# Six attention layers on one core: row tiles of TensorE that hold one head instead of two

## The chip, the cores and the metric

The kernel runs on one core of a Trainium2 chip. Its time is the device time of one execution in microseconds (us); the median of three is given for the kernel before, and lower is better.

## What is computed

A batch of 16 sequences (256 rows of 256 numbers, float32) passes through six layers. Five are attention layers with 16 heads of 16 numbers: L0 (keys and values from a context of 120 rows, with a mask, layer norm after), L1 (the same context, layer norm after), SELF (causal self-attention on 256 rows, layer norm ahead), CROSS (the context again, layer norm ahead) and L3 (the context, weights quantized to three values, layer norm ahead). Between CROSS and L3 stands FFN, two linear layers with a ReLU. Each attention layer is, for each sequence and cut to its core:

```python
q = (x @ Wq + bq).reshape(B, S, 16, 16)
k = (c @ Wk + bk).reshape(B, C, 16, 16)
v = (c @ Wv + bv).reshape(B, C, 16, 16)
scores = jnp.einsum('bqhd,bkhd->bhqk', q, k) * 16 ** -0.5
probs = jax.nn.softmax(scores, axis=-1)
ctx = jnp.einsum('bhqk,bkhd->bqhd', probs, v).reshape(B, S, 256)
y = x + ctx @ Wo + bo
```

## The kernel before, in words

An item is one sequence in one layer: i = 16 x layer + sequence, 96 items, 80 of them of attention (0 to 15 are L0, 16 to 31 L1, 32 to 47 SELF, 48 to 63 CROSS, 64 to 79 FFN, 80 to 95 L3). In the layers other than SELF two neighbouring sequences share one load, one K and one V: their contexts lie beside each other as 240 columns.

An attention item goes through named stages. On TensorE: Q (projection, L549), K and V (L560, L572), A (scores with queries on the output partitions, for the maxima; L600, in SELF L612 and L622), M (transpose of the negated maxima, L634), B (scores with keys on the output partitions, L655 and L660), PV (L679 to L689), ON, OT (transposes, L699, L709), O (output projection, L718). A has one unit for each half of the queries (SELF: three units, since the causal mask leaves one quarter out), B one for each half of the heads (SELF again three). On the other engines: Qh and Ql write the rounded part of q (fp32r) and its rest from PSUM (L794 on ACT, L917 on DVE), K0, Kh and Kl do so for k (L804 and L815 on ACT, L925 on DVE), max takes the maxima from the scores (L966 on DVE), mTe copies the transposed maxima (L823 on ACT), exp is L839 and L841 on ACT.

A score is a product in three parts, as high x high + high x rest + rest x high (PARTS, line 12), so that fp32r products keep float32's precision. The products of A and B use the array as four row tiles of 32 rows each, so that four matmuls run beside each other. 32 rows hold two heads of 16. To get one head's scores, the keys lie in SBUF twice, once with the odd heads zeroed and once with the even heads zeroed: the tensor hsel, 1 or 0 for each partition, multiplies them in Kh and Kl. A unit of A is 24 matmuls (2 groups of heads x 3 parts x 4 row tiles) that each cover two heads, 240 columns. A unit of B is 24 matmuls of 256 columns (2 heads x 3 parts x 4 row tiles), and 8 more at L660 add the negated maxima, picked out of mT by a column of ones and zeros (pickr).

```python
e.matmul(banks[j][0:n, wide * x:wide * x + wide], kz[row[j], lk, g, c, k0:k0 + n], q[row[j], lq, g, qs_],
         start=(x == 0 and y_ == 0), stop=False)
...
t = e.matmul(banks[j][0:n, wide * x:wide * x + wide], pickr[row[j], 2 * g + c:2 * g + c + 1].to_broadcast([32, n]), mt[row[j], qs_],
             start=False, stop=(x == len(parts) - 1))
```

The order on each engine is fixed at build time. make_plan lists every stage with the stages that it follows, a wanted time (WANT, in items, added to i), a length (LONG, us) and for transfers a landing time (LAND); Plan.run plays these numbers through and writes down the order in which each engine takes its stages. Buffers are rings (Slots) and PSUM banks, given out in the same play. At run time each engine goes through its list in order and waits on semaphores; nothing overtakes. SP issues all transfers, in its own list.

## Time and profile before

| | before |
|---|---|
| median of 3 executions | 1464.22 us (1463.85 to 1464.83) |
| the profiled execution: its time, its span | 1464.82 us, 1463.1 us |
| TensorE matmul (PE) busy | 1404.4 us, 96% of the span |
| DVE, ACT, POOL busy | 1005.1, 783.9, 481.4 us |
| mean granted clock of TensorE | 0.991 |
| moved by DMA | 34.79 MB, 14000 packets |

The span runs from the first to the last instruction of the program on the core. Busy is the time in which at least one instruction of the engine was under way. An fp32 matmul of the source stands as two records in the trace (L549: 640 records for 320 matmuls), an fp32r matmul as one. Matmuls of different row tiles overlap, so what a stage costs is read from the start of its first matmul to the start of the next stage's, and not from the duration of one.

### The profile page before, as it was taken

The numbers are of one execution on the slowest core, as the hardware profiler recorded it, in microseconds if no ns is written. First come the engines' busy times: TensorE is split into PE (matmuls) and PEld (weight loads), VectorE is DVE, ScalarE is ACT, GpSimd is POOL, SyncE is SP. The second block draws the span as 40 slices with busy tenths as digits, with TensorE's granted clock in tenths as the row PEclk, the third lists the DMA queues.
The fourth block names the chain that finished last, engine by engine and source line by source line (L and its number), as shares of the span: only waits on it lengthen the run. The fifth ranks groups of instructions, "written<-read, shape, count | busy, mean of one in ns | idle before, by whom it ended". The sixth has DMA issues, their size and how long they took to land.

```text
span 1463.1 us, 42292 instructions
## 1 busy us (share of the span) xinstructions
PE 1404.4 (96%) x18408; PEld 1138.3 (78%) x18408; DVE 1005.1 (69%) x1895; ACT 783.9 (54%) x1305; POOL 481.4 (33%) x511
## 2 busy tenths in 40 slices
PE   4999999999999999999999999999989999899998
PEld 3777777777777777777777777778989999677775
DVE  3667677698787776666666677778686666656664
ACT  2565655655656555555555666665423334565663
POOL 6122213344444453332332221112485555000100
PEclk8999999999999999999999999999999999999999
DMA  7101000100000000000000100000000000000000
GB/s 290 37 26 43 23 26 15 52 9 16 9 9 9 31 16 2 2 2 2 2 2 16 45 9 9 15 9 23 30 1 1 2 1 8 16 30 30 30 24 30
DMA packets 14000, 34.79 MB, mean 24 GB/s; under 512 B 2167, under 2 KB 7543, under 8 KB 12407
## 3 DMA queue, kind: packets, MB, share of 16 engines
q1 hardware_dynamic: 13815, 32.09, 6.7%
...
## 4 chain that ended last, share of the span: by engine, by line
PE 82%; DVE 8%; ACT 5%; issue 2%; DMA 1%; POOL 1%; SPq 0%; DVEq 0%; ACTq 0%; POOLq 0%
PE ps L549 10%; PE ps L718 9%; PE ps L655 7%; PE ps L682 7%; PE ps L600 6%; PE ps L731 5%; PE ps L699 5%; PE ps L572 5%; PE ps L744 5%; PE ps L560 5%; ACT s_PU L841 4%; DVE s_nm L966 4%; PE ps L660 2%; PE ps L679 2%; PE ps L539 2%
## 5 line engine op out<-in xcount | busy, mean ns | idle before, releaser
L966 DVE TENSOR_REDUCE s_nm<-ps 128x8 fp32r<-128x960 f32 (+1 forms) x352 | 395.2, 1168 | 132.8 <-PE ps L600 74.8
L841 ACT ACTIVATE s_PU<-ps 120x1024 f32<-120x1024 f32 (+1 forms) x288 | 273.1, 1028 | 161.2 <-PE ps L660 161.2
L1105 POOL TENSOR_TENSOR s_xs<-s_xs,s_rowv 128x512 f32<-128x512 f32 x96 | 126.4, 1317 | 508.8 <-DVE s_nt L909 460.9
L655 PE MATMUL ps<-s_Qs,s_KH 32*120 32x256 f32 (+2 forms) x4608 | 180.3, 286 | 5.9 <-DVE s_xs L987 2.8
L655 PEld LDWEIGHTS ps<-s_Qs,s_KH 32*120 32x120 f32 (+1 forms) x4608 | 150.3, 181 | 41.2 <-issue 31.2
L549 PE MATMUL ps<-s_xT,s_W 128*128 128x256 f32 x640 | 163.4, 399 | 10.6 <-DMA s_xT<-x_t 9.4
L850 ACT ACTIVATE s_Os<-ps 128x512 f32<-128x512 f32 x160 | 94.4, 596 | 128.5 <-PE ps L682 83.4
L718 PE MATMUL ps<-s_W,s_oT 128*128 128x256 f32 x640 | 156.6, 387 | 1.3 <-ACT s_oT L857 0.9
L794 ACT ACTIVATE s_Qs<-ps,s_colv 128x256 fp32r<-128x256 f32 x160 | 67.2, 472 | 148.5 <-PE ps L549 148.5
L549 PEld LDWEIGHTS ps<-s_xT,s_W 128*128 128x128 f32 x640 | 118.2, 195 | 35.9 <-issue 11.1
L682 PE MATMUL ps<-s_PU,s_Vp 120*32 120x256 f32 x2048 | 126.3, 383 | 6.8 <-DVE s_nm L966 5.5
L718 PEld LDWEIGHTS ps<-s_W,s_oT 128*128 128x128 f32 x640 | 115.3, 190 | 20.8 <-ACT s_oT L857 2.4
L600 PEld LDWEIGHTS ps<-s_KH,s_Qs 32*128 32x128 f32 x3072 | 99.6, 185 | 34.4 <-issue 31.0
L600 PE MATMUL ps<-s_KH,s_Qs 32*128 32x240 f32 x3072 | 123.4, 290 | 1.4 <-DVE s_nm L966 1.4
L699 PE MATMUL ps<-s_ident,s_Os 128*128 128x128 f32 x640 | 100.4, 280 | 11.5 <-ACT s_PU L841 9.5
L987 DVE TENSOR_TENSOR s_xs<-ps,s_xs 128x512 f32<-128x512 f32 x96 | 66.2, 690 | 62.7 <-PE ps L718 56.4
L917 DVE SCALAR_TENSOR_TENSOR s_Qs<-ps,s_colv,s_Qs 128x256 fp32r<-128x256 f32 x160 | 69.7, 477 | 49.7 <-ACT s_Qs L794 49.7
L869 ACT ACTIVATE s_KH<-ps,s_c 128x256 fp32r<-128x256 f32 x128 | 50.3, 476 | 98.7 <-PE ps L731 98.7
L731 PE MATMUL ps<-s_Xs,s_W1s 128*128 128x256 f32 x768 | 100.3, 287 | 2.2 <-DVE s_PU L1034 2.2
L744 PE MATMUL ps<-s_W2s,s_KH 128*128 128x256 f32 x768 | 100.4, 288 | 0.5 <-POOL s_KH L1138 0.4
L1122 POOL TENSOR_SCALAR s_rs<-s_mv 128x2 f32<-128x2 f32 x96 | 21.4, 223 | 240.2 <-DVE s_mv L1003 237.5
L1138 POOL TENSOR_TENSOR s_KH<-s_PU,s_KH 128x1024 fp32r<-128x1024 f32 x32 | 76.7, 2397 | 69.0 <-DVE s_PU L1034 68.5
...
## 6 DMA issues: line engine op xcount, KB each, us to landing
...
s_W<-w_att SPq DMA_DIRECT2D x5, 1024.0 KB, 5.0
s_xs<-x_nat SPq DMA_DIRECT2D x4, 1024.0 KB, 11.8
s_xT<-x_t SPq DMA_DIRECT2D x16, 256.0 KB, 2.7
out<-s_xs SPq DMA_DIRECT2D x16, 256.0 KB, 2.0
...
s_W<-w_ff SPq DMA_DIRECT2D x2, 1024.0 KB, 5.1
...
```

The lines of the kernel that those rows point to most:

```text
L549: t = e.matmul(m[:, g * 256:g * 256 + 256], wv(layer, 0)[:, k, 128 * g:128 * g + 128], xT_of(i)[:, k, :], start=(k == 0), stop=(k == 1))
L600: t = e.matmul(banks[j][:, 240 * g:240 * g + 240].rearrange("p (c n) -> p c n", c=2), q[row[j], lq, g, 128 * u:128 * u + 128], kz[row[j], ...
L655: e.matmul(banks[j][0:n, wide * x:wide * x + wide], kz[row[j], lk, g, c, k0:k0 + n], q[row[j], lq, g, qs_], start=(x == 0 and y_ == 0), st ...
L682: t = e.matmul(o, vp[0:C, i % 2, 32 * h:32 * h + 32], p[0:C, j // 2, at:at + 256], start=True, stop=True, tile_position=(0, 32 * j))
L699: t = e.transpose(m[:, 256 * q + 128 * gr:256 * q + 128 * gr + 128], Os[slot("Os", (i, hf))][:, gr, 128 * q:128 * q + 128], ident[:, :])
L718: t = e.matmul(m[:, 256 * q:256 * q + 256], o[:, k, 128 * q:128 * q + 128], wv(layer_of(i), 3)[:, k, :], start=(k == 0), stop=(k == 1))
L731: t = e.matmul(o, W1[:, cw, k, 128 * mt:128 * mt + 128], x[:, cx, k, :], start=(c == 0 and k == 0), stop=(c == 2 and k == 1))
L744: t = e.matmul(m[:, 256 * q:256 * q + 256], hs[:, ch, k, 128 * q:128 * q + 128], W2[:, cw, 4 * hf + k, :], start=(hf == 0 and k == 0 and c ...
L841: t = e.activation(P_of(i, k)[0:n, :, :], pair("B", i, k)[0:n, :, :], ACT.Exp, scale=0.25)
L850: e.activation(o[:, :, :].rearrange("p a n -> p (a n)"), bankM("PV", i, hf), ACT.Copy).then_inc(sem["PVe"])
L966: e.tensor_reduce(o, v, AX.X, ALU.max, negate=True).then_inc(sem["max"])
L1105: e.tensor_tensor(xs[:, b, :, :], xs[:, b, :, :], row2(layer, 0), ALU.add).then_inc(sem["pool"])
```

## The change

Each row tile of 32 rows now holds one head. Its even rows hold the rounded part of the 16 numbers, its odd rows the rest. For a head, the stationary and moving operands are taken from three layouts:

- Z: rounded q in the even rows, rest of q in the odd rows;
- Z2: rounded q in the even rows; in the odd rows zero during A, and the negated maxima during B. Z2 has four slots, which lie in the space of W2, the second weight of FFN;
- KK, two layers in KH: layer 0 has rounded k in even and odd rows, layer 1 has the rest of k in the even rows and constants of zeros and ones (pick) in the odd ones.

One product Z x KK[0] gives high x high and rest x high, a second product Z2 x KK[1] gives high x rest, and in B also adds the maximum. So a head's scores take two matmuls in place of three, and the 8 matmuls of L660 go. A unit of A is now 32 matmuls of 120 columns (4 heads x 2 products x 4 row tiles; SELF: 32 of 128 columns, then 16 of 256), a unit of B is 16 of 256 columns (SELF's third: 32 of 128).

A row of q comes from PSUM on another partition than the one it is needed on. So Qh, Ql, Kh and Kl write to a staging ring (HL, three slots, shared with the X of FFN), and transfers from SBUF to SBUF on SP lay the rows out: Qd 0 is five transfers (two to Z, two to Z2, one of zeros to Z2), Qd 1 two, Kd 0 four, Kd 1 two, and Md one, which brings the negated maxima into Z2's odd rows, four times over. Each is 128 KB for q, 120 KB for k, and 256 KB for the zeros and the maxima. That is 8 transfers for each of the 80 items and 6 for each of 48 K stages, 928 in all. A waits for Qd 1 and Kd 1, B for Md. Kp, a transfer on POOL's queue, writes the constants for items 0 and 2 and each K of L3 (10 in all). Stage K0 and the tensor hsel are gone, Kh reads PSUM. W2 is loaded into its two parts later (Wh 2 waits for the last four items of CROSS to finish B; the first Qd of L3 waits for FFN's last F2). WANT, LONG, LAND and STAY are set anew.

```diff
-        self.ring = {"Q": Slots(3), "KH": Slots(2), "K0": Slots(2), "PU": Slots(7), "Vp": Slots(2), "cT": Slots(2),
+        self.ring = {"Z": Slots(3), "Z2": Slots(4), "KH": Slots(2), "HL": Slots(3), "PU": Slots(7), "Vp": Slots(2), "cT": Slots(2),
...
             add("ACT", "Qh", after=[("Q", i, 0)])
             add("DVE", "Ql", after=[("Qh", i, 0)])
+            add("SP", "Qd", 0, after=[("Qh", i, 0)])
+            add("SP", "Qd", 1, after=[("Ql", i, 0)])
...
             add("ACT", "mTe", after=[("M", i, 0)])
+            add("SP", "Md", after=[("mTe", i, 0)])
...
             def A(i, u):
-                w.wait_ge(sem["Ql"], nth("Ql", i))
-                w.wait_ge(sem["Kl"], nth("Kl", first))
+                w.wait_ge(*dma_ops["Qd", i, 1])
+                w.wait_ge(*dma_ops["Kd", first, 1])
...
+                for x, (c, g) in enumerate(heads):
+                    for l in range(2):
+                        for j in range(4):
...
+                            t = e.matmul(banks[j][:, n * x:n * x + n], z[l][row[j], 2 * c + g, q0:q0 + 128],
+                                         kk[l][row[j], c, g, k0:k0 + n], start=(x == 0 and l == 0 and layer != "L0"),
+                                         stop=(layer != "SELF" and x == 3 and l == 1))
...
             def Bk(i, u):
-                w.wait_ge(sem["mTe"], nth("mTe", i))
-                for x, (g, c, k0, qs_) in enumerate(parts):
-                    for j in range(4):
-                        t = e.matmul(banks[j][0:n, wide * x:wide * x + wide], pickr[row[j], 2 * g + c:2 * g + c + 1].to_broadcast([32, n]), mt[row[j], qs_],
-                                     start=False, stop=(x == len(parts) - 1))
+                w.wait_ge(*dma_ops["Md", i, 0])
...
+                            t = e.matmul(banks[j][0:n, wide * x:wide * x + wide], kk[l][row[j], c, g, k0:k0 + n],
+                                         z[l][row[j], 2 * c + g, qs_], start=(x == 0 and l == 0), stop=(x == len(heads) - 1 and l == 1))
...
             def Khi(i):
-                w.wait_ge(sem["K0"], nth("K0", i))
-                for c in range(2):
-                    t = e.activation(K_of(i)[:, 0, :, c, :], K0_of(i), ACT.Copy, scale=hsel[:, c:c + 1])
+                for g in range(2):
+                    t = e.activation(k[:, g, :], m[:, g * 256:g * 256 + n], ACT.Identity, bias=bk(layer_of(i), g))
...
+            def Qd(i, k):
...
+                for c in range(2):
+                    half = f32_of(src[64 * c:64 * c + 64, :])
+                    e.dma_start(f32_of(z[k:128:2, c, :]), half).then_inc(s, 16)
+                    if not k:
+                        e.dma_start(f32_of(z2[0:128:2, c, :]), half).then_inc(s, 16)
+                if not k:
+                    w.wait_ge(sem["cst"], 5)
+                    e.dma_start(f32_of(Z2_of(i)[1:128:2, :, :]),
+                                f32_of(nought[:, :]).rearrange("p (o n) -> p o n", o=1).to_broadcast([64, 4, S])).then_inc(s, 16)
...
+            def Kd(i, k):
...
+                for c in range(2):
+                    half = f32_of(src[64 * c:64 * c + 64, :, :])
+                    for at in ((0,) if k else (0, 1)):
+                        e.dma_start(f32_of(kk[at:128:2, c, :, :]), half).then_inc(s, 16)
+
+            def Md(i):
...
+                e.dma_start(f32_of(Z2_of(i)[1:128:2, :, :]),
+                            f32_of(m[:, :]).rearrange("p (o n) -> p o n", o=1).to_broadcast([64, 4, S])).then_inc(s, 16)
```

How the new numbers move the stages shows where the waits for transfers stand. On TensorE of the kernel before, in the steady part of L3, from Q (L549) to the next unit of B (L655, L660); L634 is M, L718 is O:

```order
L549 MATMUL ps<-s_xT,s_W 128x256 x4
L709 MATMUL ps<-s_ident,s_On 128x128 x4
L634 MATMUL ps<-s_ident,s_nm 128x128 x2
L539 MATMUL ps<-s_ident,s_nt 128x128 x4
L699 MATMUL ps<-s_ident,s_Os 128x128 x4
L718 MATMUL ps<-s_W,s_oT 128x256 x4
L655 MATMUL ps<-s_Qs,s_KH 120x256 x24
L660 MATMUL ps<-s_mT,s_pickr 120x256 x8
```

Between M and B stand one T, one ON and one O. In the changed kernel, same layer, from M (L659) to B (L681); the eight rows of L640 are one unit of A, L735 is O:

```order
L659 MATMUL ps<-s_ident,s_nm 64x128 x2
L640 MATMUL ps<-s_KH,s_Z 128x120 x4
L640 MATMUL ps<-s_KH,s_W2s 128x120 x4
L640 MATMUL ps<-s_KH,s_Z 128x120 x4
L640 MATMUL ps<-s_KH,s_W2s 128x120 x4
L640 MATMUL ps<-s_KH,s_Z 128x120 x4
L640 MATMUL ps<-s_KH,s_W2s 128x120 x4
L640 MATMUL ps<-s_KH,s_Z 128x120 x4
L640 MATMUL ps<-s_KH,s_W2s 128x120 x4
L735 MATMUL ps<-s_W,s_oT 128x256 x4
L681 MATMUL ps<-s_Z,s_KH 120x256 x4
L681 MATMUL ps<-s_W2s,s_KH 120x256 x4
```

A unit of A, the first of the next item, has come between M and B. Ahead of this piece stand, from the end of Q on: half of B, K (L592), one unit of A, and then this piece of TensorE's list, which ends with M (L701 is both halves of PV, L571 T, L716 ON, L726 OT):

```order
L701 MATMUL ps<-s_PU,s_Vp 32x256 x16
L571 MATMUL ps<-s_ident,s_nt 128x128 x4
L716 MATMUL ps<-s_ident,s_Os 128x128 x4
L726 MATMUL ps<-s_ident,s_On 128x128 x4
L716 MATMUL ps<-s_ident,s_Os 128x128 x4
L659 MATMUL ps<-s_ident,s_nm 64x128 x2
```

So the new item's A stands behind these stages, where before it stood behind a whole B, T, OT, M, two ON, O and K or V as well. SP's list, which before had a load or a store at this place and nothing else, is in the same stretch of L3 (L1272, L1274 and L1277 are Qd, L1295 is Kd, L1302 is Md, L1252 the store):

```order
L1252 DMA out<-s_xs 128x512
L1272 DMA s_Z<-s_HL 64x512
L1274 DMA s_W2s<-s_HL 64x512
L1272 DMA s_Z<-s_HL 64x512
L1274 DMA s_W2s<-s_HL 64x512
L1277 DMA s_W2s<-s_nought 64x4x256
L1272 DMA s_Z<-s_HL 64x512 x2
L1295 DMA s_KH<-s_HL 64x2x240 x6
L1302 DMA s_W2s<-s_mT 64x4x256
```

Thirteen transfers for one item's q and a pair's k stand in a row, and the maxima of the item before it behind them. In L1 and CROSS the new list is wider: an item's A comes at least one whole item of TensorE work behind its Q, K's A more than one, and between M and B stand either two units of A, T, OT, V and O, or T, B's half, PV's two halves, Q and ON. In SELF, for every other item, between K and its A stand a unit of A, Q, both halves of PV, two ON, M and V.

## Rows read from the trace of the kernel before

**Rows 1.** The page: the chain that ended last, shares of the span by engine

```profile
PE 82%; DVE 8%; ACT 5%; issue 2%; DMA 1%; POOL 1%; SPq 0%; DVEq 0%; ACTq 0%; POOLq 0%
```

**Rows 2.** Busy time by stretch: L1, SELF, L3, and the sum of six stretches

```profile
core 0: us, PE busy (x) PEld busy (x) DVE busy (x) ACT busy (x) POOL busy (x), PEclk, DMA share, GB/s
...
250.00:470.00 220.00, 215.48 (x2976) 170.91 (x2972) 177.00 (x364) 128.42 (x211) 92.36 (x108) 1.00 0.06 18
470.00:810.00 340.00, 336.22 (x4841) 258.99 (x4844) 225.21 (x389) 188.16 (x294) 127.81 (x160) 1.00 0.03 9
...
1240.00:1463.00 223.00, 209.14 (x2923) 162.93 (x2921) 136.00 (x222) 128.03 (x207) 14.33 (x13) 0.98 0.08 27
sum 1463.00, PE 1404.41 PEld 1138.32 DVE 1005.12 ACT 783.89 POOL 481.45; mean PE 234.07 PEld 189.72 DVE 167.52 ACT 130.65 POOL 80.24
```

**Rows 3.** Timeline of TensorE in SELF: start, us from start to end, line, shapes, count

```profile
620.95 0.97 PE L622 MATMUL ps<-s_KH,s_Qs 32*128 32x512 f32 x12
621.86 0.61 PE L625 MATMUL ps<-s_cbf,s_idb 128*128 128x256 bf16 x4
...
632.96 0.88 PE L655 MATMUL ps<-s_Qs,s_KH 32*128 32x256 f32 x24
633.67 0.40 PE L660 MATMUL ps<-s_mT,s_pickr 32*128 32x256 f32 x8
...
636.58 1.56 PE L655 MATMUL ps<-s_Qs,s_KH 32*128 32x128 f32 x48
637.97 0.61 PE L660 MATMUL ps<-s_mT,s_pickr 32*128 32x128 f32 x16
638.42 0.93 PE L612 MATMUL ps<-s_KH,s_Qs 32*128 32x256 f32 x24
```

**Rows 4.** Timeline of L3, rows of TensorE

```profile
1363.57 0.60 PE L709 MATMUL ps<-s_ident,s_On 128*128 128x128 f32 x4
1364.00 0.60 PE L539 MATMUL ps<-s_ident,s_nt 128*128 128x128 f32 x4
...
1365.14 1.99 PE L718 MATMUL ps<-s_W,s_oT 128*128 128x256 f32 x8
...
1367.07 0.97 PE L655 MATMUL ps<-s_Qs,s_KH 32*120 32x256 f32 x24
...
1367.85 0.42 PE L660 MATMUL ps<-s_mT,s_pickr 32*120 32x256 f32 x8
...
1368.09 0.89 PE L655 MATMUL ps<-s_Qs,s_KH 32*120 32x256 f32 x24
...
1371.72 0.94 PE L600 MATMUL ps<-s_KH,s_Qs 32*128 32x240 f32 x24
...
1372.59 1.93 PE L682 MATMUL ps<-s_PU,s_Vp 120*32 120x256 f32 x32
...
1374.46 0.94 PE L600 MATMUL ps<-s_KH,s_Qs 32*128 32x240 f32 x24
```

**Rows 5.** Groups by line on ACT and DVE: count, busy us, mean ns, idle before

```profile
L794 ACT ACTIVATE s_Qs<-ps,s_colv 128x256 fp32r<-128x256 f32 x160 | 67.2, 472 | 148.5 <-PE ps L549 148.5
L823 ACT ACTIVATE s_mT<-ps 128x256 fp32r<-128x256 f32 x80 | 31.6, 395 | 26.4 <-PE ps L634 26.3
L925 DVE SCALAR_TENSOR_TENSOR s_KH<-s_K,s_hsel,s_KH 128x480 fp32r<-128x480 f32 (+1 forms) x96 | 77.5, 848 | 3.0 <-ACT s_KH L815 3.0
```

**Rows 6.** Timeline of SP's queue at the start: two issues in a row

```profile
1.23 0.43 SPq L1177 DMA_DIRECT2D s_ident<-ident  x1
1.70 0.42 SPq L1177 DMA_DIRECT2D s_caus<-causal  x1
```

**Rows 7.** DMA issues: KB each, median us from issue to landing

```profile
s_W<-w_att SPq DMA_DIRECT2D x5, 1024.0 KB, 5.0
s_xT<-x_t SPq DMA_DIRECT2D x16, 256.0 KB, 2.7
out<-s_xs SPq DMA_DIRECT2D x16, 256.0 KB, 2.0
```

More of the change, by code:

```diff
@@ L238, in make_plan @@
         if layer == "FFN":
-            add("DVE", "X", after=[x_t], rings=[("X", i, [("F1", i, 1)])])
+            add("DVE", "X", after=[x_t], rings=[("HL", ("X", i), [("F1", i, 1)])])
             for u in range(2):
@@ L313, in make_plan, with layer_end @@
                 add("POOL", "rs", 1, after=[("st", i, 1)])
-    def layer_end(layer, name): return [(name, B * LAYERS.index(layer) + b, 0) for b in range(B)]
+    def layer_end(layer, name, k=0): return [(name, B * LAYERS.index(layer) + b, k) for b in range(B)]
     p.add("SP", "w", "L0", want=-9)
@@ L337, in make_plan @@
         for c in range(4):
-            p.add("ACT", "Wh", n, c, want=50 + 5 * (n - 1) + c, after=[("w", layer, 0)])
-            p.add("POOL", "Wl", n, c, want=50.5 + 5 * (n - 1) + c, after=[("Wh", n, c)])
+            p.add("ACT", "Wh", n, c, want=50 + 14 * (n - 1) + .1 * c, after=[("w", layer, 0)] + ([("Wh", 2, 0)] if n == 2 and c else []),
+                  rings=[("Z2", ("W2", s), layer_end("FFN", "F2", 1)) for s in range(4)] if n == 2 and not c else [])
+            p.add("POOL", "Wl", n, c, want=50.5 + 14 * (n - 1) + .1 * c, after=[("Wh", n, c)])
     for m in range(4):
@@ L873, in Wh @@
                 w.wait_ge(sem[f"d_wF{n}"], 16)
+                if n == 2:
+                    for s in range(4):
+                        was = ring["Z2"].before["W2", s]
+                        w.wait_ge(sem["B"], max(nth("B", was, u) for u in range(units(was))))
                 src = W[WSLOT[f"F{n}"]][:, 512 * c:512 * c + 512]
@@ L1228, in _ @@
             for name, i, k in plan.order["SP"]:
-                do[name](i)
+                if name in do:
+                    do[name](i)
+                else:
+                    part[name](i, k)
             e.wait_ge(sem["d_out"], 16 * B)
```

292 lines of the change are left out of this document (161 added, 131 removed).

## The prediction

> **What bounds the kernel now.** The chain that ended last goes through TensorE for 82% of the span [rows 1]. The stretches say the same of every layer: in L1 TensorE is busy for 215.5 of 220 us, in SELF for 336.2 of 340, while DVE is busy for 177 and 225, ACT for 128 and 188 [rows 2]. Only L3, with 209 of 223 us, has idle time worth the name. ACT's and DVE's groups sit idle until TensorE is done (148.5 us ahead of L794 alone, [rows 5]). So a microsecond of TensorE work removed is a microsecond of time, as long as the other engines and the transfers still deliver in time; work removed on ACT and DVE is worth nothing by itself. The timelines of TensorE give the price of each stage, from its start to the next stage's.
>
> **The price of four row tiles.** A group is four matmuls, one for each row tile, that run beside each other. Groups of 128 columns: 48 matmuls from 636.58 to 637.97 are 12 groups in 1.39 us, 0.116 us each, and the 16 of L660 behind them take 0.45 us, 0.113 each [rows 3]. Groups of 256 columns: six in 0.71 us, 0.118 each [rows 3], and the two of L660 0.24 us, 0.12 each [rows 4]. Groups of 512 columns: 0.91 us for three [rows 3]. A unit of A of 240 columns takes 0.87 us, 1371.72 to 1372.59 [rows 4]: six groups at 0.116 and 0.17 us for getting in and out. So up to 256 columns a group costs the same whatever its width: **what counts is the number of matmuls, not of columns.**
>
> **What TensorE gains, part by part.**
> - B outside SELF, 2 units for each of 64 items, 128 units. A unit loses two of its six groups of L655 (2 x 0.118) and both of L660 (0.24): 0.476 us, in all 61 us.
> - B in SELF, first and second unit (32): the same 0.476, 15 us. Third unit (16): from 16 groups of 128 columns to 8, 8 x 0.114 = 0.91, in all 15 us.
> - A in SELF, second and third unit (32): three groups of 512 columns in 0.91 us become four of 256, 4 x 0.118 + 0.17 = 0.64. 0.27 us each, 9 us.
> - A outside SELF (128 units): 24 matmuls of 240 columns become 32 of 120. Two more groups are 2 x 0.116 = +0.23 us, the upper bound. The lower one: the 48 matmuls of 128 columns took 1.39 us, only 0.04 over twelve groups at 0.113 [rows 3], so eight and that little entry are 0.94, +0.07 against 0.87. I take the middle, +0.15: **19 us are lost** (9 to 29). A's first unit in SELF goes the same way, 16 x 0.15 = 2 us.
>
> Sum: 61 + 15 + 15 + 9 - 19 - 2 = 79 us less on TensorE (67 to 90).
>
> Here the Trainium skill speaks otherwise. Its page "TensorE: Matmul & The Clock Gate" (Back-to-back issue gap) has the gap between matmuls follow the columns, N / 2.4 + 2.5 ns, which would make A cheaper by the change; the same page (LDWEIGHTS) gives a load of P columns P / 1.2 ns, 107 ns for 128, whatever the rows. The trace's 0.113 us a group at 128 columns agrees with the second and not with the first.
>
> **ACT and DVE.** K0 and the doubled Kh go, Kl shrinks from 848 ns for an instruction over 480 columns [rows 5] to about what Ql's take. This hides under TensorE and I count zero. It is what keeps DVE, 80% busy in L1 [rows 2], at about that share of a shorter item.
>
> **What the transfers add.** Two issues in a row on SP start 0.47 us apart [rows 6]. 928 transfers are 436 us of SP, a third of the span: SP is not the bound, but each chain through it is long. From issue to landing 256 KB took 2.0 us out of SBUF and 2.7 us into it [rows 7]; that these transfers stay within SBUF no row shows, so I bound them by these two and take 2.7, since they come in bunches as the loads do.
> - *q and k in L3.* After Q: Qh 2 x 0.472 = 0.94 us [rows 5], then thirteen issues, the last one starting 12 x 0.47 = 5.64 us later, and 2.0 to 2.7 us: 8.6 to 9.3 us. Over it the order leaves half of B (4 x 0.118 + 0.17 = 0.64), K (as O, 1.93, less its 240 columns: 1.8), a unit of A (1.02), PV (1.87), T, two ON and OT at 0.43 each, and M (some 0.25): 7.3 us [rows 4]. A is late by 1.3 to 2.0 us. Eight times: 16 us. The other eight items have no k: 0.94 + 6 x 0.47 + 2.7 = 6.5 us, hidden.
> - *Maxima in L3.* mTe 0.40 us [rows 5], handing over 0.1, landing 2.0 to 2.7, and ACT may first have to finish a copy: 2.5 to 3.5 us, against one unit of A and O, 1.02 + 1.93 = 2.95 [rows 4]. I take 0.5 us late, 16 times: 8 us.
> - *SELF*, every second K: the issues of the next item's Qd stand between Kd 0 and Kd 1. Not worse than in L3, at least nothing: 1.0 us, 8 times, 8 us (0 to 16).
> - *L1 and CROSS*: a whole item of TensorE work over q and k, over 5 us over the maxima. Nothing, as long as landing stays under 4 us.
> - *FFN to L3*: the first Qd waits for the last F2, and 27 transfers, 12.7 us of issuing, must go out before the third item's A. The order covers some of it with projections and transposes: 8 us (2 to 12). *Start*: 33 transfers, 15.5 us, before the third A, but the first A stands behind seven projections: 3 us (-3 to 8). CROSS to FFN (late W2) and the end: 1 us each.
>
> Sum 16 + 8 + 8 + 8 + 3 + 2 = 45 us (9 to 65).
>
> **The number.** The profiled execution took 1464.8 us, 0.6 above the median. 1464.8 - 79 + 45 = 1430.8; against the median, **1430 us**, 2.3% faster.
>
> **The rivals.**
> - *The waits are hidden.* The transfers land in 2 us, and what is late moves to where TensorE has other work queued. Only the fill of L3 and the start cost, 12 us: 1464.2 - 79 + 12 = 1397 us. For it: SP is mostly idle. Against it: TensorE takes nothing out of order. 17%.
> - *Transfers inside SBUF are slow, and the kernel gets slower.* Place: the bunches of Qd and Kd in L3 and SELF. Their volume is 4 x 128 + 256 + 2 x 128 KB for q, 1024 KB, and 720 KB for k. 1024 KB landed in 5.0 us [rows 7], about 340 KB/us once 2 us are taken off; thirteen transfers, 1744 KB, then need 5.1 us, less than their issuing. If they move markedly slower, each bunch lands x us later still. That costs 16x for the 16 late bunches above, 16(x - 1) for the other 16 items of L3 and SELF, which have about 1 us of slack, and half of x for each of L3's 16 maxima, 40x - 16 in all. From x = 1.25 us the gain is gone; at 2 us the time is 1430 + 64 = 1494 us. For it: sources are halves of the partitions, and nothing in the trace shows such a transfer. 20%, of which a fifth ends within 0.2% of no change.
> - *Cost goes by columns after all.* A group of 120 columns would cost 0.055, a unit of A 8 x 0.055 + 0.17 = 0.61 us, 0.41 less than I take: 128 x 0.41 = 52 us, 1378 us. This is what the skill's gap rule (same page as above) would give. The rows of 128 columns are against it: 3%.
>
> **How the numbers follow.** My forecast, 1410 to 1455, has 60%. A measurement of this kernel can tell 0.2%, 3 us, from no change. Faster: 60 + 17 + 3 = 80%; same 4%; slower 16%. The range goes from TensorE's upper gain with the least waits, 1464 - 90 + 10, about 1385, to x = 1.7 in the slow rival, 1482.
>
> **What would show it.** In the profile after: the start of a unit of B to the next stage's 0.48 us shorter; a unit of A 0.07 to 0.23 longer; PE busy near 1330; in L1 and CROSS 12.9 to 13.2 us for an item and few waits; PE rows in L3 that wait for a DMA into KH, Z or W2s, 2 us at every second A; from issue to landing of Qd and Kd 2 to 3 us. The prediction is wrong in its mechanism if L1 or CROSS show such waits too, if landing takes over 4 us, or if A's unit gets shorter.

## The result, and the profile after

The changed kernel takes **1619.6 us** (median of 4 executions, 1609.5 to 1621.6), 155 us more than the kernel before, which ran beside it at 1464.1. The ratio is 1.105 (1.100 to 1.109). The forecast was 1430 us with a range of 1385 to 1482: wrong in sign, and outside the range. The profiled execution took 1621.6 us. Its page, with the chain that ended last under the busy times:

```profile
span 1619.9 us, 39900 instructions
PE 1432.4 (88%) x16616; PEld 1123.7 (69%) x16616; DVE 974.8 (60%) x1895; ACT 728.6 (45%) x1209; POOL 484.9 (30%) x521
DMA packets 131754, 178.34 MB, mean 110 GB/s; under 512 B 16887, under 2 KB 87799, under 8 KB 130167
...
PE 51%; SPq 13%; ACT 10%; DMA 10%; DVE 7%; issue 6%; POOL 3%; ACTq 0%; POOLq 0%; DVEq 0%
```

TensorE has 1792 matmul records fewer than before (18408 there), and yet it is busy 28 us longer (1404.4 before). Its share of the chain fell from 82% [rows 1] to 51%, and SP's queue (SPq) and transfers (DMA) took 13% and 10%. By stretch (columns as in [rows 2]; the start with L0, L1, SELF, and from the middle of FFN to the end):

```profile
0.00:250.00 250.00, 197.55 (x2332) 149.84 (x2336) 131.46 (x263) 96.39 (x148) 63.93 (x75) 0.90 0.62 167
250.00:470.00 220.00, 206.92 (x2678) 156.88 (x2674) 162.78 (x337) 118.00 (x188) 83.19 (x98) 1.00 0.60 138
470.00:810.00 340.00, 306.25 (x3742) 226.70 (x3740) 212.56 (x391) 157.76 (x247) 119.57 (x148) 0.96 0.45 102
...
1240.00:1619.00 379.00, 329.06 (x3438) 267.48 (x3437) 190.44 (x348) 154.34 (x274) 70.17 (x57) 0.91 0.38 93
```

The granted clock is 0.90 in the first stretch and 0.91 in the last, where [rows 2] had 0.98 for L3. The waits of TensorE, the longest sums (us in total, times, longest):

```profile
PE ps L681 <- DMA s_W2s<-s_mT: 36.3, 29, 4.1
PE ps L640 <- issue: 32.1, 12, 4.8
PE ps L581 <- DMA s_xT<-x_t: 23.7, 2, 15.4
PE ps L571 <- DVE s_nm L983: 10.8, 17, 0.7
PE ps L640 <- DMA s_Z<-s_HL: 10.0, 6, 5.4
```

B (L681) waits for the maxima, A (L640) for q and k. The wait of L581 is that of the first Q for its load at the start. After the start, the longest single waits stand at the bunches of thirteen transfers in L3. SP's queue at one of them (start, us, line, copy, count):

```profile
1523.89 0.46 SPq L1272 DMA_DIRECT2D s_Z<-s_HL  x1
1524.40 0.60 SPq L1274 DMA_DIRECT2D s_W2s<-s_HL  x1
1525.04 0.60 SPq L1272 DMA_DIRECT2D s_Z<-s_HL  x1
1525.68 0.60 SPq L1274 DMA_DIRECT2D s_W2s<-s_HL  x1
1526.32 0.62 SPq L1277 DMA_DIRECT2D s_W2s<-s_nought  x1
1526.98 1.50 SPq L1272 DMA_DIRECT2D s_Z<-s_HL  x2
1528.53 3.88 SPq L1295 DMA_DIRECT2D s_KH<-s_HL  x6
1532.46 0.61 SPq L1302 DMA_DIRECT2D s_W2s<-s_mT  x1
```

Two issues start 0.64 us apart, not 0.47 as two loads did at the start [rows 6]. The six Kd of L1295 take 3.88 us, so the last starts at about 1528.53 + 5 x 0.655 = 1531.8. It lands 2.4 us later, at 1534.2, and that lets A go. TensorE in the same piece:

```profile
1530.09 0.38 PE L659 MATMUL ps<-s_ident,s_nm 128*64 128x128 f32 x2
1534.23 0.33 PE L640 MATMUL ps<-s_KH,s_Z 32*128 32x120 f32 x4 [3.77 <-issue]
1534.36 0.31 PE L640 MATMUL ps<-s_KH,s_W2s 32*128 32x120 f32 x4
...
1535.27 3.61 PE L735 MATMUL ps<-s_W,s_oT 128*128 128x256 f32 x8
1538.81 0.41 PE L681 MATMUL ps<-s_Z,s_KH 32*120 32x256 f32 x4
```

After M (L659) TensorE stands idle for 3.77 us. The trace names "issue" (no releaser that it shows), but A's first matmul starts as the last Kd lands. Then O (L735, eight records) takes 3.61 us, where the same eight took 1.99 before [rows 4]. The same piece in stretches of 3 us (TensorE busy first, the last three columns are granted clock, share of the DMA engines, GB/s) says why:

```profile
1527.00:1530.00 3.00, 3.00 (x40) 2.14 (x32) 3.00 (x6) 2.12 (x5) 0.00 (x0) 1.00 0.95 200
1530.00:1533.00 3.00, 0.47 (x5) 0.16 (x3) 1.27 (x5) 0.89 (x2) 1.25 (x1) 1.00 0.87 215
1533.00:1536.00 3.00, 1.77 (x34) 1.65 (x35) 0.54 (x1) 0.00 (x0) 0.00 (x0) 0.91 0.65 139
1536.00:1539.00 3.00, 3.00 (x11) 1.90 (x14) 1.76 (x3) 0.00 (x0) 0.00 (x0) 0.52 0.00 0
1539.00:1542.00 3.00, 3.00 (x40) 2.32 (x40) 0.61 (x1) 2.35 (x4) 0.00 (x0) 1.00 0.23 87
```

After the idle time the clock falls to its lower level (0.52 is 1.2 of 2.4 GHz for nearly all of the 3 us) and comes back. In the slow stretch the DMA engines are idle (0.00), so it isn't their traffic that slows O. So one late bunch is paid twice, 3.8 us idle and 1.6 us in O. From issue to landing (KB each, median us):

```profile
s_Z<-s_HL SPq DMA_DIRECT2D x320, 128.0 KB, 3.0
s_KH<-s_HL SPq DMA_DIRECT2D x192, 120.0 KB, 2.4
s_W2s<-s_HL SPq DMA_DIRECT2D x160, 128.0 KB, 2.5
s_W2s<-s_nought SPq DMA_DIRECT2D x80, 256.0 KB, 3.3
s_W2s<-s_mT SPq DMA_DIRECT2D x80, 256.0 KB, 3.2
```

In L1 TensorE waits 0.8 us for transfers, its clock is 1.00, and it was slower all the same. There a unit of B and a unit of A read so (the start of what comes next stands in the last row of each):

```profile
425.00 0.38 PE L681 MATMUL ps<-s_Z,s_KH 32*120 32x256 f32 x4
...
425.76 0.47 PE L681 MATMUL ps<-s_Z,s_KH 32*120 32x256 f32 x4
...
432.84 0.33 PE L640 MATMUL ps<-s_KH,s_Z 32*128 32x120 f32 x4
433.00 0.28 PE L640 MATMUL ps<-s_KH,s_W2s 32*128 32x120 f32 x4
...
433.88 0.66 PE L716 MATMUL ps<-s_ident,s_Os 128*128 128x128 f32 x4
```

B's unit takes 0.76 us (0.66 in L3) and A's 1.04 (0.87 before, [rows 4]). Both are near the forecast (0.64 and 1.02). What is missing lies in the rest of the item. Over ten items of L1, TensorE is busy with A and B for 3.53 us of an item, 4.07 before: 0.54 us less. But it is idle for 0.71 us of each item, 0.31 before, and the other stages, the same work as before, keep it busy for 0.37 us more. The longest sum of its waits in this stretch is one for DVE, where the maxima (L983) were the last thing done:

```profile
PE ps L571 <- DVE s_nm L983: 5.7, 8, 0.7
```

How long an item takes is read in this study from M's transposes, one M per item, over a steady piece: in L1 from the layer's item 4 to its item 14, in SELF 2 to 14, in CROSS 4 to 12, in L3 6 to 14 (counted from 0). For L3, eight items between the first and last start, in the kernel before (count of records, ns, first and last start):

```profile
L634 PE MATMUL ps<-s_ident,s_nm x18: 272/285/329, 1323.5 to 1432.1; 128*128 128x128 f32 x18
```

And in the changed kernel:

```profile
L659 PE MATMUL ps<-s_ident,s_nm x18: 272/273/300, 1443.2 to 1585.5; 128*64 128x128 f32 x18
```

That is 13.56 and 17.77 us for an item (the very last record is M's second; the first of its pair starts 0.1 to 0.2 us sooner). Such a piece is not the whole layer, and another piece can read some tenths otherwise: experiment 9's L3 is 13.40 in this one and 14.07 two items earlier. All kernels of the study, by the same reading:

| us for an item | L1 | SELF | CROSS | L3 | whole kernel |
|---|---|---|---|---|---|
| before | 13.83 | 21.05 | 13.56 | 13.56 | 1464.2 |
| after | 14.07 | 22.62 | 14.23 | 17.77 | 1619.6 |
| in place, order of after | 14.04 | 20.75 | 14.15 | 13.09 | 1485.8 |
| in place, wants of before | 14.21 | 20.68 | 14.30 | 13.96 | 1474.8 |
| before, wants of after | 14.26 | 21.50 | 14.27 | 13.92 | 1499.1 |
| after, transfers planned at true length | 14.04 | 20.64 | 14.09 | 13.58 | 1514.5 |
| after, fillers in L3 | 14.10 | 22.55 | 14.17 | 16.71 | 1607.3 |
| after, no zeros | 14.13 | 21.76 | 14.15 | 16.96 | 1579.0 |
| after, a quarter of the zeros | 14.07 | 22.02 | 14.15 | 17.48 | 1601.2 |
| after, true lengths and new order | 13.33 | 21.23 | 13.33 | 13.04 | 1494.4 |
| before, true lengths and new order | 13.92 | 21.32 | 14.07 | 13.40 | 1487.7 |
| in place, true lengths and new order | 12.98 | 19.86 | 12.92 | 12.96 | 1412.3 |
| after, true lengths and new order, no zeros | 13.32 | 21.01 | 13.33 | 13.02 | 1473.1 |

### The profile page after: what moved, and what is told of

Read it like the earlier page. It is cut to its first block, busy times and chain, and to the rows that moved or that the text cites. A ratio compares the mean times of both kernels' runs of the same rounds, so it can differ in the third digit from the quotient of the medians.

```text
span 1619.9 us, 39900 instructions
## 1 busy us (share of the span) xinstructions
PE 1432.4 (88%) x16616; PEld 1123.7 (69%) x16616; DVE 974.8 (60%) x1895; ACT 728.6 (45%) x1209; POOL 484.9 (30%) x521
## 2 busy tenths in 40 slices
DMA packets 131754, 178.34 MB, mean 110 GB/s; under 512 B 16887, under 2 KB 87799, under 8 KB 130167
## 4 chain that ended last, share of the span: by engine, by line
PE 51%; SPq 13%; ACT 10%; DMA 10%; DVE 7%; issue 6%; POOL 3%; ACTq 0%; POOLq 0%; DVEq 0%
DMA s_W2s<-s_mT 6%; PE ps L735 6%; PE ps L581 6%; PE ps L701 6%; PE ps L640 5%; PE ps L761 5%; PE ps L748 5%; ACT s_PU L853 5%; SPq L1272 5%; PE ps L681 5%; PE ps L604 4%; SPq L1295 4%; PE ps L716 3%; PE ps L592 3%; SPq L1274 3%
## 5 line engine op out<-in xcount | busy, mean ns | idle before, releaser
L983 DVE TENSOR_REDUCE s_nm<-ps 128x8 fp32r<-128x960 f32 (+1 forms) x352 | 394.8, 1167 | 126.7 <-PE ps L640 67.4
L640 PE MATMUL ps<-s_KH,s_Z 32*128 32x120 f32 (+2 forms) x2560 | 179.0, 303 | 48.8 <-issue 32.1
L640 PEld LDWEIGHTS ps<-s_KH,s_Z 32*128 32x128 f32 x2560 | 140.3, 200 | 83.5 <-issue 66.7
L581 PE MATMUL ps<-s_xT,s_W 128*128 128x256 f32 x640 | 165.0, 404 | 23.8 <-DMA s_xT<-x_t 23.7
L735 PE MATMUL ps<-s_W,s_oT 128*128 128x256 f32 x640 | 167.8, 408 | 6.3 <-ACT s_oT L869 6.0
L681 PE MATMUL ps<-s_Z,s_KH 32*120 32x256 f32 (+2 forms) x1536 | 125.2, 330 | 53.0 <-DMA s_W2s<-s_mT 36.3
L640 PE MATMUL ps<-s_KH,s_W2s 32*128 32x120 f32 (+2 forms) x2560 | 167.8, 286 | 0.0
L681 PEld LDWEIGHTS ps<-s_Z,s_KH 32*120 32x120 f32 (+1 forms) x1536 | 83.0, 189 | 109.3 <-issue 56.6
L581 PEld LDWEIGHTS ps<-s_xT,s_W 128*128 128x128 f32 x640 | 121.9, 201 | 50.4 <-issue 18.0
L735 PEld LDWEIGHTS ps<-s_W,s_oT 128*128 128x128 f32 x640 | 125.6, 202 | 29.1 <-ACT s_oT L869 6.8
L701 PE MATMUL ps<-s_PU,s_Vp 120*32 120x256 f32 x2048 | 135.9, 390 | 7.5 <-ACT s_PU L853 5.4
L640 PEld LDWEIGHTS ps<-s_KH,s_W2s 32*128 32x128 f32 x2560 | 141.5, 201 | 0.2
L1134 POOL TENSOR_SCALAR_AFFINE_SELECT s_PU<-s_PU 128x512 f32<-128x512 f32 (+1 forms) x96 | 77.1, 803 | 212.8 <-ACT s_PU L853 206.6
L933 DVE SCALAR_TENSOR_TENSOR s_HL<-ps,s_colv,s_HL 128x256 fp32r<-128x256 f32 x160 | 69.7, 477 | 98.1 <-ACT s_HL L818 98.1
L818 ACT ACTIVATE s_HL<-ps,s_colv 128x256 fp32r<-128x256 f32 x160 | 67.6, 479 | 96.8 <-PE ps L581 95.7
L991 DVE RECIPROCAL s_Rc<-ps 128x16 f32<-128x16 f32 x160 | 40.5, 253 | 114.6 <-PE ps L716 110.4
L716 PE MATMUL ps<-s_ident,s_Os 128*128 128x128 f32 x640 | 103.2, 285 | 5.9 <-ACT s_PU L853 3.3
```

The costliest lines, as they stand in the source:

```text
L581: t = e.matmul(m[:, g * 256:g * 256 + 256], wv(layer, 0)[:, k, 128 * g:128 * g + 128], xT_of(i)[:, k, :], start=(k == 0), stop=(k == 1))
L640: t = e.matmul(banks[j][:, n * x:n * x + n], z[l][row[j], 2 * c + g, q0:q0 + 128], kk[l][row[j], c, g, k0:k0 + n], start=(x == 0 and l == ...
L681: t = e.matmul(banks[j][0:n, wide * x:wide * x + wide], kk[l][row[j], c, g, k0:k0 + n], z[l][row[j], 2 * c + g, qs_], start=(x == 0 and l ...
L701: t = e.matmul(o, vp[0:C, i % 2, 32 * h:32 * h + 32], p[0:C, j % 2, at:at + 256], start=True, stop=True, tile_position=(0, 32 * j))
L716: t = e.transpose(m[:, 256 * q + 128 * gr:256 * q + 128 * gr + 128], Os[slot("Os", (i, hf))][:, gr, 128 * q:128 * q + 128], ident[:, :])
L735: t = e.matmul(m[:, 256 * q:256 * q + 256], o[:, k, 128 * q:128 * q + 128], wv(layer_of(i), 3)[:, k, :], start=(k == 0), stop=(k == 1))
```

## The experiments

**1. No transfers at all, the order as it is.** Qh, Ql, Kh and Kl write Z and KH in place, A waits for Ql and Kl, B for mTe. Order, matmul shapes and ACT's and DVE's work are those of the changed kernel.

```diff
-                w.wait_ge(*dma_ops["Qd", i, 1])
-                w.wait_ge(*dma_ops["Kd", first, 1])
+                w.wait_ge(sem["Ql"], nth("Ql", i))
+                w.wait_ge(sem["Kl"], nth("Kl", first))
...
-                w.wait_ge(*dma_ops["Md", i, 0])
+                w.wait_ge(sem["mTe"], nth("mTe", i))
...
+            def Qd(i, k): pass
```

> The changed kernel without its transfers in SBUF: Qh, Ql, Kh and Kl write where the products read, A waits for Ql and Kl and B for mTe, and both products of a head read these same tiles. Matmuls, shapes and the order on every engine are those of the changed kernel. Left out: the row layout, zeros, maxima and constants, so scores are not the reference's and exp uses a scale of 0.001. Theory 1 (waiting for transfers, and the clock that falls while TensorE waits, cost all of it): the time comes down to my forecast without waits, 1464 - 79 = 1385 to 1400 us. Theory 2 (waits and clock cost most, but the new order also costs, since L1 shows 14.07 us for an item at full clock with hardly a wait for a transfer): 1440 to 1480 us, and L1 still at about 14.0 us an item. Theory 3 (traffic in SBUF slows TensorE's own reads): L1 falls below 13.5 us an item with the same order.

Measured: 1485.8 us (1484.9 to 1486.6), ratio 1.014 (1.013 to 1.016). So in this order the transfers and what hangs on them cost 1619.6 - 1485.8 = 134 us, most of the loss. But 21 us of loss stay without a single one of them: the 79 us that TensorE should gain didn't show either. L3 came to 13.09 us for an item, near the 12.9 of the forecast; L1 and CROSS stayed at 14.0 to 14.2. This is theory 2, a little over its range.

**2. The same with the old wants.** The transfer stages are taken out of the plan as well, and WANT and STAY are those of before.

```diff
-WANT = dict(xT=-3, cT=-4, mi=-4, bo=-2.63, N=0.86, T=-0.91, Te=-0.73, Q=-0.27, Qh=3.92, Ql=-0.83, K=-0.27, Kh=2.72, Kl=0.19,
+WANT = dict(xT=-3, cT=-4, mi=-4, bo=-0.9, N=0.88, T=-0.79, Te=-1.18, Q=0.15, Qh=3.01, Ql=-0.26, K=-0.32, Kh=1.79, Kl=0.17,
-            add("SP", "Md", after=[("mTe", i, 0)])
```

> As the first, but without the transfer stages in the plan and with the wanted times (WANT, STAY) of the kernel before, so that the order is close to that of before. Theory 1: same as the first run, 1385 to 1400 us. Theory 2: here the saving of 79 us on TensorE shows whole, 1385 to 1405 us, 40 us or more under the first run. Theory 3: same as the first run.

Measured: 1474.8 us (1473.3 to 1476.0), ratio 1.006 (1.005 to 1.008), 11 us less than experiment 1: no theory had that. The old wants don't give the old order either, since the plan plays other stages with them. In the steady piece of L1 the array changes between row tiles, column tiles (PV) and whole 8.7 times for an item, in the kernel before 6.0 times, and TensorE is busy for 13.79 us of an item, before 13.52. So this run doesn't show what the new form would do in the order of before.

**3. The kernel before with the new wants.**

```diff
-WANT = dict(xT=-3, cT=-4, mi=-4, bo=-0.9, N=0.88, T=-0.79, Te=-1.18, Q=0.15, Qh=3.01, Ql=-0.26, K=-0.32, Kh=1.79, Kl=0.17,
+WANT = dict(xT=-3, cT=-4, mi=-4, bo=-2.63, N=0.86, T=-0.91, Te=-0.73, Q=-0.27, Qh=3.92, Ql=-0.83, K=-0.27, Kh=2.72, Kl=0.19,
-STAY = 0.121
+STAY = 0.153
```

> The kernel before, planned with the wanted times and STAY of the changed kernel (K0 at 2.6), nothing else changed. Theory 2 (the order costs by itself): slower than before by 30 to 60 us, near 1500 us. Theories 1 and 3: within 8 us of before, 1456 to 1472 us.

Measured: 1499.1 us (1498.2 to 1501.6), ratio 1.024 (1.022 to 1.025). With the same instructions, another order costs 34 us (1465.2 for the kernel before beside it). L1 and CROSS go to 14.26 and 14.27 us for an item, as in the changed kernel, and TensorE is idle for 0.89 us of an item in L1. So their miss comes with the order and not with the transfers.

**4. The changed kernel, with a plan that knows how long its transfers take.** Only the numbers of the plan differ: five lengths and two landing times get longer, the landing of Kd gets shorter.

```diff
-Qd=.4, Kd=.4, Kp=1.3, Md=.08
+Qd=3.3, Kd=2.6, Kp=1.3, Md=.65
-LAND = dict(Kp=3.0, Qd=2.2, Kd=2.6, Md=2.1,
+LAND = dict(Kp=3.0, Qd=2.7, Kd=1.9, Md=2.6,
-            add("SP", "Qd", 1, after=[("Ql", i, 0)])
+            add("SP", "Qd", 1, after=[("Ql", i, 0)], long=1.3)
-                add("SP", "Kd", 1, after=[("Kl", i, 0)])
+                add("SP", "Kd", 1, after=[("Kl", i, 0)], long=1.3)
```

> The changed kernel, planned with the lengths its trace shows: 0.65 us for the issue of a transfer (Qd 3.3 and 1.3, Kd 2.6 and 1.3, Md 0.65) and 1.9 to 2.7 us to land, in place of 0.4, 0.4, 0.08. If A and B come too early in L3 and SELF because the plan held issuing to be almost free, the time falls to 1520 to 1580 us and L3 from 17.8 to under 16 us an item. If the waits come from SP's queue whatever the plan, it stays above 1600 us.

Measured: 1514.5 us (1512.4 to 1516.5), ratio 1.034 (1.032 to 1.036). That is 105 us less, with all 928 transfers still there, and 29 us more than experiment 1 has without them. The plan had held the five issues of Qd 0 as 0.4 us, where SP needs some 5 x 0.65 = 3.25, and so put A where its operands could not be. L3 falls from 17.77 to 13.58 us for an item; L1 stays at 14.04.

**5. Is the falling clock a cost of its own?** Fillers (bf16 matmuls of 512 columns into A's own banks, 14 or 3 of them) run ahead of A's wait in L3. They add work and take no wait away.

```diff
+                if layer == "L3" and u == 0:
+                    w.wait_ge(sem["cst"], 3)
+                    empty("A", i, 0)
+                    for n_ in range(3 if i % 2 else 14):
+                        e.matmul(banks[n_ % 2].rearrange("p (r n) -> p r n", r=4), idb[:, :],
```

> The changed kernel with filler work on TensorE: in L3, ahead of the wait for an item's q and k, 14 (even items) or 3 (odd items) bf16 matmuls of 512 columns into the banks that A overwrites right after, about 3.0 and 0.65 us at full clock, less than the waits of 3.8 and 1.2 to 1.5 us there. If the clock that falls during the wait costs time of its own (O behind it takes 2.91 us an item in place of 1.88), L3 gets shorter by 1.0 to 1.6 us an item and the kernel by 15 to 25 us although work is added. If the loss is the wait alone, the time stays within 3 us of the changed kernel's or rises.

Measured: 1607.3 us (1605.1 to 1611.1), ratio 1.097 (1.095 to 1.100), 12 us less than the changed kernel, under the 15 to 25 expected; L3 takes 16.71 us for an item, 1.06 less. The executions of the changed kernel differ by 12 us among themselves, but only one of its four (1609.5) lies within the range of this one. TensorE in L3 of this kernel, L619 being the fillers, L665 M, L646 A, L741 O:

```profile
1525.85 0.38 PE L665 MATMUL ps<-s_ident,s_nm 128*64 128x128 f32 x2
1526.07 3.19 PE L619 MATMUL ps<-s_cbf,s_idb 128*128 128x512 bf16 x14
1530.75 0.33 PE L646 MATMUL ps<-s_KH,s_Z 32*128 32x120 f32 x4 [1.49 <-issue]
...
1531.79 1.99 PE L741 MATMUL ps<-s_W,s_oT 128*128 128x256 f32 x8
```

From M to A it is now 4.9 us (4.1 in the changed kernel), so the wait itself got no shorter, but O is back at 1.99. From L3's first M to the end the granted clock is 0.98, in the changed kernel 0.89. The clock is a cost of its own, about 1 us for an item in L3, and its cause is the idle time.

**6 and 7. Issues or bytes?** The transfer of zeros (256 KB behind each Qh) is left out, or made a quarter as large. Z2 is set to zero once at the start instead, so that both leave out the zeros that A needs later.

```diff
-                    e.dma_start(f32_of(Z2_of(i)[1:128:2, :, :]),
-                                f32_of(nought[:, :]).rearrange("p (o n) -> p o n", o=1).to_broadcast([64, 4, S])).then_inc(s, 16)
...
+                    e.dma_start(f32_of(Z2_of(i)[1:128:2, 0, :]), f32_of(nought[:, :])).then_inc(s, 16)
```

(The last line stands in 7 alone.)

> The changed kernel without the fifth transfer of Qd 0 (the zeros), so 80 issues and 20 MB less; Z2 is set to zero once at the start. Left out: Z2's odd rows are not zero during A, so the maxima are not the reference's, and exp uses a scale of 0.001. If SP's issuing is the chain (0.65 us each), L3 gets shorter by 0.65 us an item or more, with some clock back, in all 12 to 30 us, and L1 and CROSS, where TensorE hardly waits for a transfer, by nothing. If waits for transfers are not what L3 hangs on, nothing changes.

> As the last, but the fifth transfer stays, with a quarter of its bytes (64 KB in place of 256 KB): the number of issues is the changed kernel's, the bytes are nearly those of the last run. If issuing on SP is the price, the time is the changed kernel's within 5 us; if the bytes are (DMA engines 95% busy at 200 GB/s in the bunches), it comes down as far as the last run.

Measured: without it 1579.0 us (1569.3 to 1583.7), ratio 1.077 (1.072 to 1.081), 41 us less, more than the 12 to 30 expected. With a quarter of the bytes 1601.2 us (1591.2 to 1608.4), ratio 1.093 (1.087 to 1.098), 18 us less. These intervals are wide, 6 to 8 us to either side, but the order is plain: three quarters of the bytes are worth about 18 us, the issue with the last quarter about 22. It is neither SP alone nor the bytes alone. That fits the stretches above, where the DMA engines are busy for 0.87 to 0.95 of the time at 200 to 215 GB/s. By an estimate from these two rates the 1744 KB of a bunch need 8.3 to 8.9 us, about as long as its thirteen issues (13 x 0.65 = 8.5). The Trainium skill ("DMA: Bandwidth & Descriptors", Where 436 GB/s comes from) gives 435 GB/s as the ceiling between two places of SBUF. These transfers come nowhere near it: the engines are all but full at half of it or less, with packets of 1.35 KB on average over the whole kernel (131754 of them). Why, no run here shows.

**8. The changed kernel, planned anew.** As in 4, and the lengths of the main stages too are those of the trace. WANT (not shown) and STAY were searched for them on the plan's own play.

```diff
...
+LONG.update(Q=1.83, K=1.68, V=1.8, O=1.85, T=0.44, ON=0.46, OT=0.44, M=0.25, F1=2.9, F2=2.9, max=1.16, exp=1.03, Te=1.05, Qh=0.95, Ql=0.95, PVe=0.6, OTe=0.6, mTe=0.4)
-STAY = 0.153
+STAY = 0.558
```

> The changed kernel planned with measured lengths for transfers and for the main stages of every engine, and with wanted times searched anew for that plan. If what the change lost beyond its matmuls is a matter of where A and B stand in the order, this comes to 1440 to 1480 us, under the fourth run's 1514, and the transfers are nearly hidden. If they can't be hidden by any order, it stays above 1500.

Measured: 1494.4 us (1488.8 to 1497.6), ratio 1.019 (1.017 to 1.022), between what was expected if order is all (1480 at most) and if no order helps (over 1500). The steady pieces of L1, CROSS and L3 are now under the kernel before, by 0.5, 0.2 and 0.5 us for an item, and it still loses. Its waits name the maxima, the start (L590, L625) and the entry of L3 (L638):

```profile
PE ps L679 <- DMA s_W2s<-s_mT: 18.4, 15, 2.3
PE ps L590 <- DMA s_cT<-ctx_t: 17.5, 1, 17.5
PE ps L625 <- DMA s_Z<-s_HL: 6.4, 1, 6.4
...
PE ps L638 <- DMA s_Z<-s_HL: 5.3, 2, 5.1
```

**9. The kernel before, planned anew in the same way** (WANT not shown).

```diff
...
+LONG.update(Q=1.83, K=1.68, V=1.8, O=1.85, T=0.44, ON=0.46, OT=0.44, M=0.25, F1=2.9, F2=2.9, max=1.16, exp=1.03, Te=1.05, Qh=0.95, Ql=0.95, PVe=0.6, OTe=0.6, mTe=0.4)
-STAY = 0.121
+STAY = 0.161
```

> The kernel before, its stage lengths set to what its trace shows and its table of wants searched anew for them, as was done for the tuned version of the change (1494 us). If the search itself is worth something here, the gap between the two forms is larger than it looked. Theory: the order of before was near its best, 1450 to 1465 us. Rival: the lengths of before were as wrong as those of the change, and the search gives 15 us or more, under 1450. Other side: the planner's model misses what the chip does (time for switching between the ways of splitting the array), and the new order is slower, over 1470.

Measured: 1487.7 us (1487.6 to 1487.7), ratio 1.016 (1.014 to 1.018). It went to the other side: what the plan takes for a gain made this kernel 23 us slower. With these lengths the plan's own play ends at 1495 us for the old wants and at 1472 for the new; the chip took 1464 and 1488. A play that is wrong by 15 to 30 us can't choose between orders that differ by 20.

**10. What the new form alone can bring.** The kernel of 2, in place and without transfers, with the lengths of 8 for the main stages and with wants (not shown) searched for this kernel.

```diff
...
+LONG.update(Q=1.83, K=1.68, V=1.8, O=1.85, T=0.44, ON=0.46, OT=0.44, M=0.25, F1=2.9, F2=2.9, max=1.16, exp=1.03, Te=1.05, Qh=0.95, Ql=0.95, PVe=0.6, OTe=0.6, mTe=0.4)
-STAY = 0.121
+STAY = 0.279
```

> Operands of one head to a row tile, the rounded parts and rests written in place and no transfer at all, with measured stage lengths and a table of wants searched for them. It is what TensorE's new form alone can bring. (The q, k and maxima that it multiplies are not laid out as the products need them, and exp has another scale, so its values are not the reference's.) Theory: the forecast of 79 us less on TensorE was right for the form, and only orders that were not made for it hid it: 1395 to 1425 us. Rival: stages cost more to get in and out of, whatever the order, and half of the 79 us was never there: 1430 to 1455 us. Second rival: nothing is left of it, 1460 or more.

Measured: **1412.3 us** (1410.2 to 1413.0), ratio 0.964 (0.963 to 0.966), 52 us less than before. L1, CROSS and L3 take 12.98, 12.92 and 12.96 us for an item; the forecast was 12.9 to 13.2. Its page says of the engines:

```profile
PE 1348.4 (96%) x16616; PEld 1089.4 (77%) x16616; DVE 970.4 (69%) x1895; ACT 725.9 (51%) x1209; POOL 477.7 (34%) x511
```

And the timeline of TensorE in its L3 (L627 A, L646 M, L722 O, L668 B, L688 PV):

```profile
1334.01 1.11 PE L627 MATMUL ps<-s_KH,s_Z 32*128 32x120 f32 x32
1335.05 0.41 PE L646 MATMUL ps<-s_ident,s_nm 128*64 128x128 f32 x2
1335.29 1.89 PE L722 MATMUL ps<-s_W,s_oT 128*128 128x256 f32 x8
1337.12 0.74 PE L668 MATMUL ps<-s_Z,s_KH 32*120 32x256 f32 x16
1337.78 1.93 PE L688 MATMUL ps<-s_PU,s_Vp 120*32 120x256 f32 x32
```

A's unit is 1.04 us (forecast 1.02), B's 0.66 (forecast 0.64). TensorE is busy 56 us less than before, and in L1 it is idle for 0.07 us of an item. The gain of the form is real, and of the three orders tried only the one searched for it shows it. Since it doesn't lay out q, k and the maxima, this is no kernel that could be used: it shows what the matmuls are worth.

**11. The planned-anew kernel of 8 without its zeros** (the edit of 6 on the kernel of 8, cut).

```diff
...
-                many = (2 if k else 5) if name == "Qd"
+                many = (2 if k else 4) if name == "Qd"
...
```

> The tuned version of the change (1494 us) without the transfer of zeros: four transfers instead of five behind each Qh, 64 issues and 16.8 MB fewer. (Where zeros are missing the products take in what lies there, and exp has another scale, so its values are not the reference's.) In the change as it was, leaving it out took 41 us off. Theory: with an order that holds transfers at their true cost they are mostly hidden, and this gives 5 to 15 us: 1480 to 1490. Rival: what is left of the loss is still the transfers in all their length, in proportion 41/134 of what they cost: 20 us or more, under 1475. Second rival: they are fully hidden, 1490 to 1500.

Measured: 1473.1 us (1471.9 to 1477.9), ratio 1.007 (1.005 to 1.008), 21 us less than experiment 8. The transfers left out are 80, not the 64 of the expectation. Half of their 41 us is left with the better order; this is the rival's size, 20 us or more, and not the 5 to 15 that I expected. So this order hides about half of what the zeros cost in the first one. How much of the other transfers it hides is not shown by this run.

No version that computes all of the reference came under the kernel before, and experiment 11, which leaves out the zeros, didn't either.

## Where the 155 us went

Three differences, each between two kernels that ran, add up to it:

| | us |
|---|---|
| the form alone, each with its order (experiment 10 less before) | 1412.3 - 1464.2 = -52 |
| the transfers, in the best order found for them, and what that order costs against the one of 10 (8 less 10) | 1494.4 - 1412.3 = +82 |
| the order of the change against that one (after less 8) | 1619.6 - 1494.4 = +125 |
| sum | +155 |

Of the last 125 us, 105 come from the numbers of the plan that hold the transfers too short (after less 4). The rest is between other orders. The 82 us can't be split into transfers and order by these runs: 8 and 10 have wants of their own.

Where in the kernel the time lies is read from M as well, in the profiled executions: from the start to the first M, then from each layer's first M to the next layer's, CROSS to its last M, and FFN from there to L3's first M:

| us | start | L0 | L1 | SELF | CROSS | FFN | L3 and end |
|---|---|---|---|---|---|---|---|
| before | 39.9 | 216.1 | 225.4 | 332.4 | 209.6 | 225.7 | 214.0 |
| after | 46.4 | 250.1 | 229.5 | 361.7 | 224.7 | 243.2 | 264.4 |
| 1, in place | 45.2 | 222.0 | 228.5 | 326.0 | 215.9 | 232.4 | 213.1 |
| 4, true lengths | 48.6 | 229.9 | 228.5 | 332.5 | 209.2 | 240.1 | 224.6 |
| 8, planned anew | 48.1 | 218.2 | 221.3 | 332.0 | 212.3 | 241.6 | 213.7 |
| 10, in place, planned anew | 44.2 | 207.8 | 220.5 | 302.8 | 207.1 | 225.5 | 203.4 |

L3 is the largest part of the loss (50 us), but L0 is the second (34 us), and the prediction had no term for it. There TensorE waited 13.6 us for the maxima and the granted clock was 0.92 (0.99 before). SELF lost 29 us. Experiment 8 has these three back to the size of before; what it still loses is the start (8 us) and, most of all, the stretch from CROSS through FFN to L3's first A (16 us), where it is no better than the changed kernel. Against experiment 10 its 76 us are SELF 29, FFN 16, L0 and L3 10 each, and 10 for the rest.

## Why the prediction was wrong

The step that failed is the first one, "a microsecond of TensorE work removed is a microsecond of time", together with a price for waiting of 45 us. The matmuls did get cheaper, but the new order made TensorE wait and gave the gain back (+21 us without any transfer, experiment 1). And in that order the transfers cost 134 us (after less 1) where 45 were taken. In detail:

- **The matmul prices held.** A group of 120 columns takes 0.11 us and one of 256 takes 0.12, so up to 256 columns cost goes by matmuls and not by columns; that rival is out. A unit of A went up by 0.17 us (0.15 taken), one of B outside SELF is 0.66 us in L3 (0.64 taken) and 0.76 in the rows of L1 above. The gap rule of the Trainium skill ("TensorE: Matmul & The Clock Gate", Back-to-back issue gap), weighed in the prediction, would have A cheaper; the page gives it for a single matmul by itself and says that in a stream the weight loads count too. The 0.17 us more speak against its use here once again.
- **"A microsecond of TensorE work removed is a microsecond of time"** failed. Without any transfer the same work gave +21, +10 and -52 us in three orders (experiments 1, 2, 10). In the last of them the sum of 79 us was right for a steady item of L1, CROSS and L3 (0.6 to 0.85 us less, 0.66 taken), and too large for SELF: 21.05 to 19.86 is 1.2 us for an item where (15 + 15 + 9 - 2) / 16 = 2.3 were taken. There TensorE's busy time fell from 20.85 to 19.36 us, and its idle time rose by 0.3; B alone was busy 1.3 us less, where 1.9 were taken. I priced stages and not the order, although the diff replaced the whole table that makes it. No rival had it. The two kernels held a sign of it: with the lengths that each was given, the plan's own play ends at 1407 us for the kernel before and at 1429 us for the changed one, 21 us the other way.
- **L1 and CROSS at 12.9 to 13.2 us** failed for that reason: 14.07 and 14.23, with the full clock in L1 and 0.8 us of waits for transfers. In L1 the 0.54 us that A and B gave are gone in 0.40 us more of idle time, waits for DVE and ACT above all, and 0.37 us more in the other stages. The kernel before with these wants shows the same 14.3. The sum counted ACT and DVE as nothing, with DVE 80% busy in L1.
- **The bunches in L3** were the right place with a price too low. Cover: M ended 7.5 us after Q's end, 7.3 were taken. Chain: from Q's end (1522.8) to the last landing (1534.2) it took 11.4 us, 8.6 to 9.3 were taken. Of the 2.5 us, 12 x 0.18 = 2.2 are the issues, which I priced by the only two plain rows at hand, loads of another shape (0.47 against 0.65). A was late by 3.8 us and not by 1.3 to 2.0. The items without a k, taken as hidden, were late by 1.2 and 1.5 us in the two cases beside this one.
- **The maxima** cost 36.3 us in all, 29 times. In L3 it was 7.6 us, the 8 of the forecast; what was missing is L0 (13.6 us), SELF (9.5) and CROSS (4.3), where they were counted as hidden or not at all. They land in 3.2 us and queue behind the other issues: in the bunch of L3, M started at 1530.09 and Md's issue at 1532.46.
- **The granted clock** was not in the sum at all. It fell to its lower level behind the stall; experiment 5 shows this as some 1 us for an item of L3, and the mean over the kernel went from 0.991 to 0.945.
- **The slow rival** (20%) had the place and the sign, and part of the mechanism: its x was time by which a bunch lands later because transfers inside SBUF are slow, with 1494 us at 2 us. The 340 KB/us that it read from one row was 200 to 215 in the bunches, but the landing times, 2.4 to 3.3 us, are within 0.6 of what I took, and the time went far past 1494. Neither the issue price nor the clock nor the order was in it.
- **PE busy near 1330** failed: 1432. Matmuls at the lower clock are busy for longer, as O above. Without transfers, in the same order and with the clock at 0.98, it is 1383 (experiment 1), in the order of experiment 10 it is 1348.

What stays open: why the searched order of experiment 10 suits the new form and the like-made one of experiment 9 doesn't suit the old; how much of the 82 us a better order than mine could still hide; what makes the stretch from CROSS to L3 16 us longer in experiment 8, of which one wait for a transfer at the entry of L3 (5.1 us) is a third; and what the new form would take in exactly the order of before, which no run has.
